# A four-layer decoder on one core: the order of semaphore waits, and constants ahead of logarithms

## The reference

```
x = layernorm(x + sublayer(x, ctx))
```

## Time and profile before

| | |
|---|---|
| median of three runs | 983.69 us (982.82 to 988.83) |
| the profiled execution | 984.17 us, of which the span of its instructions is 982.1 us |
| instructions in the span | 22255 |
| mean clock granted to TensorE | 0.936 of full speed |

### The profile page before, as it was taken

The page is one execution under the profiler, slowest core; times in us unless marked ns, Lnnn a source line. Parts: engine busy times, 40 slices in busy tenths (PEclk is TensorE's granted clock), DMA queues, the critical chain, the costliest instruction groups (busy, mean ns, idle before and its releaser), DMA issues. The chain is left out here.

```text
span 982.1 us, 22255 instructions
## 1 busy us (share of the span) xinstructions
PE 851.2 (87%) x9160; PEld 676.4 (69%) x9160; DVE 550.2 (56%) x1631; ACT 451.1 (46%) x923; POOL 50.5 (5%) x71
## 2 busy tenths in 40 slices
PE   7679799899989997898888979989998989998772
PEld 5247778688878785676566757877887867786551
DVE  4843565663466476357735964655425647564455
ACT  2045243454544683585264234243375446433443
POOL 2300000010010000001000000001001000000000
PEclk9689989999999998998897999999999999999965
DMA  9100000401000301103000000040100030000000
GB/s 342 62 2 2 2 1 1 172 2 38 1 20 1 146 2 43 46 12 145 2 13 1 2 2 2 1 173 1 39 2 20 1 145 2 1 1 2 2 2 21
DMA packets 6837, 36.23 MB, mean 37 GB/s; under 512 B 721, under 2 KB 4305, under 8 KB 5458
## 3 DMA queue, kind: packets, MB, share of 16 engines
q1 hardware_dynamic: 6738, 34.81, 9.6%
HBM read 34.28 MB, written 0.52 MB: 35 GB/s over the span
## 5 line engine op out<-in xcount | busy, mean ns | idle before, releaser
L697 PE MATMUL bank<-xT,weights_F 128*128 128x256 f32 x832 | 203.0, 386 | 3.1 <-ACT p L1844 2.6
L697 PEld LDWEIGHTS bank<-xT,weights_F 128*128 128x128 f32 x832 | 152.0, 193 | 26.9 <-issue 4.2
L705 PEld LDWEIGHTS bank<-weights_F,p 128*128 128x128 f32 x1088 | 133.4, 191 | 19.5 <-DVE p L1390 8.1
L705 PE MATMUL bank<-weights_F,p 128*128 128x128 f32 x1088 | 141.5, 278 | 4.3 <-DVE p L1390 3.7
L1769 ACT ACTIVATE p<-bank 128x512 f32<-128x512 f32 x160 | 84.3, 603 | 78.3 <-PE bank L517 78.2
L1709 ACT ACT_TABLE_LOAD x76 | 97.5, 1283 | 13.2 <-DMA weights_con<-in_con 6.5
L1374 DVE SCALAR_TENSOR_TENSOR res<-bank,comb,res 128x128 f32<-128x128 f32 x184 | 55.6, 344 | 64.5 <-PE bank L705 62.2
L1844 ACT ACTIVATE p<-bank 128x512 f32<-128x512 f32 x72 | 42.4, 597 | 91.4 <-PE bank L697 91.1
L1207 DVE TENSOR_REDUCE m_wide<-bank 128x4 f32<-128x512 f32 x96 | 60.2, 682 | 39.3 <-PE bank L803 29.6
L1390 DVE TENSOR_TENSOR p<-p,bank 128x512 f32<-128x512 f32 x72 | 49.2, 684 | 45.7 <-PE bank L697 26.7
L1920 ACT ACTIVATE p<-bank 128x512 f32<-128x512 f32 x64 | 36.5, 598 | 52.8 <-PE bank L697 52.6
(11 more groups left out here) (311 smaller groups left out, 1363.7 us busy)
## 6 DMA issues: line engine op xcount, KB each, us to landing
weights_F<-in_L1f SPq DMA_DIRECT2D x2, 4096.0 KB, 13.0
weights_F<-in_L0f SPq DMA_DIRECT2D x2, 3456.0 KB, 12.4
weights_F<-in_L2f SPq DMA_DIRECT2D x2, 3456.0 KB, 12.2
weights_Y<-in_L1x_kv SPq DMA_DIRECT2D x2, 1024.0 KB, 10.3
weights_Z<-in_L1x SPq DMA_DIRECT2D x2, 1024.0 KB, 11.4
weights_Y<-in_L2a SPq DMA_DIRECT2D x2, 898.0 KB, 4.5
weights_Z<-in_L2x SPq DMA_DIRECT2D x2, 449.0 KB, 3.2
weights_con<-in_con SPq DMA_DIRECT2D x1, 692.5 KB, 4.9
```

The source lines that it names most:

```text
L697: m = mm(b[:, k * NT:(k + 1) * NT], W[weight][:, f:f + P], s.xT[:], start=True, stop=True)
L705: m = mm(b[:, tk(u)], h[:, tk(u)], w, start=k == 0, stop=k == len(chunks) - 1)
```

## The change

Three edits, none of which changes what stands in `TURN_ORDER` or how many waits there are.

1. At many places the `wait_ge` calls of one instruction are written in another order, so that another of them comes first. In loops over four banks the last bank is now named first.
2. The epsilons and the one are given as immediate numbers in the instruction. The last layer's own logarithm (L2337) keeps its column.
3. A call of `exp_ln()` stands ahead of the exponential at L2004.

```
                 def turn_x(st):
+                    pe.wait_ge(*told("x_new", NS))
                     b = opened("act", st, "xT")
-                    pe.wait_ge(*told("x_new", NS))
...
                 def project(st, w, outs=None):
+                    for a in (outs or [(st, "o", u) for u in range(NS)])[::-1]:
+                        pe.wait_ge(*freed(*a))
                     b = opened("dve", st, "y")
-                    for a in outs or [(st, "o", u) for u in range(NS)]:
-                        pe.wait_ge(*freed(*a))
...
                 def turn_maxima(st, u):
+                    pe.wait_ge(*told("maxima"))
                     b = opened("dve", st, "mT", u)
-                    pe.wait_ge(*told("maxima"))
...
                     for u in range(NS):
-                        for i in range(4):
+                        for i in (3, 2, 1, 0):
                             pe.wait_ge(*freed(st, "t", u, 0, i))
                         values8(st, u, [(0, probs_at(4 * u))])
...
                     pe.wait_ge(*weights("con"))
+                    pe.wait_ge(*told("L0a_qs"))
                     b = opened("act", "L0a", "qsT")
-                    pe.wait_ge(*told("L0a_qs"))
...
-                def add_product(st, base, name="y"):
-                    b = bank(st, name)
+                def add_product(st, base, b, name="y"):
                     link(dve.tensor_tensor(s.res[:], by_sample(b[:, 0:NT]), base[:], ALU.add), free(st, name))
...
                 def tail(st, base=None, before=None):
 
+                    b = bank(st, "y")
                     if base is None:
                         dve.wait_ge(*told("xb"))
                         base = s.xb
-                    add_product(st, base)
+                    add_product(st, base, b)
...
-                    for i in range(4):
+                    for i in (3, 2, 1, 0):
                         dve.wait_ge(*freed(st, "s", u, 0, i))
                     in_parts(u)
...
                 def divided(st, u):
+                    dve.wait_ge(*told("inverse"))
                     b = bank(st, "o", u)
-                    dve.wait_ge(*told("inverse"))
...
                         if e < 9:
+                            dve.wait_ge(*freed(st, "gate", e))
+                            up = bank(st, "up", e)
                             if e >= 3:
                                 bank(st, "y", e - 3)
-                            dve.wait_ge(*freed(st, "gate", e))
-                            o.count(dve.tensor_tensor(s.p[:, 2 + e % 3], s.p[:, e % 2], bank(st, "up", e)[:], ALU.mult),
-                                    free(st, "up", e))
+                            o.count(dve.tensor_tensor(s.p[:, 2 + e % 3], s.p[:, e % 2], up[:], ALU.mult), free(st, "up", e))
...
-            eps5, eps6, one, eps8 = (const("eps")[:, i:i + 1] for i in range(4))
+            eps5, eps6, eps8 = 1e-5, 1e-6, 1e-8
...
+                    exp_ln()
                     act.wait_ge(*told("L3x_absf"))
                     link(act.activation(gt[:, 5], gt[:, 5], ACT.Exp))
-                    o.count(act.activation(gt[:, 5], gt[:, 5], ACT.Ln, bias=one[0:64]), sem("L3x_softplus"))
+                    o.count(act.activation(gt[:, 5], gt[:, 5], ACT.Ln, bias=1.0), sem("L3x_softplus"))
```

More of the change, by code:

```diff
@@ L668, in L0x @@
                     yield
-                    for blk in range(2):
-                        for i in range(4):
+                    for blk in (1, 0):
+                        for i in (3, 2, 1, 0):
                             pe.wait_ge(*freed("L0x", "t", 0, blk, i))
@@ L917, in L2a @@
                     yield
+                    pe.wait_ge(*freed("L2a", "kv"))
+                    for c in (1, 0):
+                        pe.wait_ge(*freed("L2a", f"qf{c}"))
                     b = opened("dve", "L2a", "o")
-                    pe.wait_ge(*freed("L2a", "kv"))
-                    for c in range(2):
-                        pe.wait_ge(*freed("L2a", f"qf{c}"))
                     for part in range(2):
@@ L943, in L2a @@
                     pe.wait_ge(*ready("L2x"))
+                    for c in (2, 0):
+                        pe.wait_ge(*freed("L2a", f"h{c}"))
                     b = opened("dve", "L2a", "y2")
-                    for c in range(0, 4, 2):
-                        pe.wait_ge(*freed("L2a", f"h{c}"))
                     for u in range(NS):
@@ L1025, in L3a @@
                     for u in range(NS):
-                        for n in range(4):
+                        for n in (3, 2, 1, 0):
                             pe.wait_ge(*freed("L3a", "t", u, 0, n))
@@ L1220, in block_maxima @@
                     if blk:
-                        for k in range(2):
+                        for k in (1, 0):
                             dve.wait_ge(free(st, "s", u, k, 3), ring.freed((pair, st, "s", u, k, 3))[1])
```

40 lines of the change are left out of this document (21 added, 19 removed).

## The result

| | before | after |
|---|---|---|
| median | 984.77 us (4 runs) | 968.28 us (4 runs, 965.15 to 971.24) |
| ratio | | 0.9851, 95% interval 0.9818 to 0.9884 |
| the profiled execution | 984.17 us | 968.22 us |
| mean clock granted to TensorE | 0.936 | 0.948 |

The changed kernel is 1.5% faster. A second series of runs gave 0.9858 [0.9807, 0.991]. The forecast of 975.6 was 7.3 us too high: the result lies inside the full range (967.2 to 982.3) and outside the forecast's own 970 to 980. The gain was 16.5 us between the medians where 8.1 was forecast. The ratios compare fast runs alone and leave out nine that lay over 1.5% above the fastest of their kernel; the differences at an equal clock, further down, have them in, and without them only that of DVE's waits moves by more than 0.5 us (to 3.5 from 2.9).

The account below looks back on a forecast made before the run. PE was taken as the bound, busy 851.2 of 982.1 us. Tails 3.5, maxima 2.2, other places 0.8 and 0.2, and table load 1.4 made 8.1 us: median 975.6, own range 970 to 980, full range 967.2 to 982.3.

Parts of the forecast that it names:

- What the links cost: Start after the late producer: 0.03 us on DVE, 0.06 on PE; logarithm about 203 ns; L697's idle 0.7 us.
- The sum: Links right behind PE's own waits count in full: tails 3.5, maxima 2.2, others 0.8 and 0.2, table load 1.4: 8.1 us.
- Waits of PE: At L456, L491, L750, L549 and L473, 43 places at 0.06 us each: 2.6 us.
- Waits of DVE: DVE's share of the tails and of the maxima: 2.7 us.
- Immediates: Logarithms at 16 tails ahead of L456, 0.09 us each: 1.4 us counted, of 6.3 on ACT in all.
- The 8.4 between the two sums: Gains between 8.1 us and the full count of 16.5, taken as hidden where PE works for the other stream.
- Table load: First turn, ahead of L2005: one load goes, 1.29 us, with the immediate 1.38, all of it reaching PE.
- PE's busy time should stay at about 851: Sign for the changed profile: only PE's idle falls, to about 123 us; busy time moving over 5 us means the clock.
- The clock: Rival: denser PE is granted less, 0.93 between 700 and 900 us, 13.9 us longer, 989.5 us; chance 0.07.
- Everything counts: Rival: every shortened wait and instruction counts, whether PE waits behind or not, 16.5 us, 967.2 us; chance 0.20.
- Absorbed: Rival: other late work takes up the gains, only the table load and a little remains, 982.3 us; chance 0.20.
- Theory A: Expectation for the first runs: hand-overs alone make the gain, terms priced too low by half, the clock is noise.

Follow-up runs that it names:

- the eight filled places: Matmuls of constants in PE's four idle times ahead of L750, in two kernels: the changed kernel 961.56 us (0.9773), the kernel before 983.45 us (0.9979).

## Why the prediction was right or wrong

- **What the links cost: right.** 0.03 to 0.04 on DVE and 0.05 to 0.06 on PE with the late wait on the instruction, as read from the earlier trace rows; 206 ns for a logarithm against 203; L697's idle 0.82 against 0.7.
- **The sum: right at an equal clock, in part by luck.** 8.1 forecast, 8.7 (1.5) measured. Its terms were not all right. Waits of PE 2.6, measured 5.9 (1.4): "L750 (4), L549 (6) and L473 (3), 13 places: 0.06 x 13 = 0.8" is too small where more than one wait instruction stood ahead, and some 60 places gained, not 43. Waits of DVE 2.7, measured 2.9 (1.4). Immediates 1.4, measured 3.8 (1.4): "The 8.4 between the two sums lie where PE is at work for the other stream. I count them as hidden": for some of the logarithms that failed. Table load 1.4, measured 1.9 (1.4), and 1.28 in the trace. Measured each alone, the parts come to 5.9 + 2.9 + 3.8 + 1.9 = 14.5, far more than the whole's 8.7. So two errors cancel: terms that were low, and an overlap of the edits that the sum does not have. What the overlap is, no run shows.
- **The step that failed: "PE's busy time should stay at about 851".** It fell to 841.0, by 10.2, more than the 5 us that the prediction itself names as the mark of the clock. The clock stood there as a rival, but only as a loss and only between 700 and 900 us. It was a gain, between 401 and 584 us, where the earlier trace rows already showed 0.93: there was something to win there, and in the stretches at 1.00 nothing. About 7 of the 16 us are this (0.0096 more of mean clock between the means of 8 and 78 runs, at 7.5 us for 0.01).
- **The chances.** "Everything counts" came nearest in time (967.2) and was not what happened: at an equal clock its 16.5 us are twice the measured, and that they equal the 16.5 between the medians is chance. By its own marks (below 973.9 is faster) the result is "faster", which had 0.38, and not "same", which had 0.58. "Absorbed" is out: PE's idle fell by 5.7 us. Theory A is out too, as PE's idle (5.7 us less) and its hand-overs (about 4) can't carry 16.
- **Not shown:** why the clock of this version is better. The edits alone have 0.941, 0.940 and 0.933, the whole 0.948. At L750 the slow stretch at the idle time is gone in six of the eight filled places and shorter in one, so there the two belong together, though stretches with no filled place just ahead of them went as well; which of the other idle times set one off, and why the whole avoids them between 401 and 584 us, was not found.

## What to carry to other kernels

Put the wait for the producer that comes last on the instruction itself: here that was worth 0.06 to 0.07 us for one wait instruction, 0.10 for two on VectorE, and up to 0.18 where TensorE waited for four semaphores, but it arrived only where the engine behind was idle. Before summing such microseconds, look up the stretches with a granted clock below 1.00 and count them as a term that can go either way; when a small, certain gain measures as a loss, compare the runs' clocks before undoing the edit. Idle times of some 2 us on TensorE can be filled with matmuls of constants, but the effect has to be measured on the whole program: it was 7 to 9 us in one version here and nothing in the other.

## What the runs showed of the hardware

- One kernel's mean granted clock differed from run to run, with a standard deviation of 0.005 around 0.938 over 78 runs of before, and its time with it, from 974.36 to 994.69 us. That is more than any single edit here is worth.
- The two semaphores of one wait instruction were not equal at L1391: late in the first place 136 ns to the start of the VectorE instruction, in the second 94 ns; on the instruction itself 38.
- Behind an idle time of 2 us TensorE was at 1.2 GHz for a while in one profile and not in the other, in the same piece of the program (0.60 against 1.00).
